# Two graph attention layers on one core: the landing of a gathered chunk awaited by each step's own chunk, on another engine

## The chip, the cores and the metric

The kernel runs on one core of one Trainium2 chip. The metric is the device time of one execution in microseconds, the median of the runs. The core has TensorE (PE), VectorE (DVE), ScalarE (ACT), GpSimd (POOL) and SyncE (SP), each with an instruction queue of its own, and they wait for each other by semaphores. Sixteen DMA engines move data between HBM and the on-chip memories, SBUF and PSUM.

## The reference

There are 3125 nodes with 128 features and 50000 edges (src, dst), sorted by dst. The dst are drawn as the whole part of 3125 u², u uniform, so low nodes have many edges and high ones few. Two layers of the same form follow each other, and at the end a layer norm over x + out:

```python
q = (x @ qw + qb).reshape(N, 2, 128); k, v likewise
alpha = einsum('ehd,ehd->eh', q[dst], k[src]) / sqrt(128)
ex = exp(alpha - segment_max(alpha, dst)[dst])
w = ex / (segment_sum(ex, dst)[dst] + 1e-16)
out = segment_sum(w * v[src], dst).mean(heads) + x @ sw + sb + x @ lin_w + lin_b
```

## The kernel before

Edges are taken in 391 chunks of 128, nodes in 49 groups of 64 (half bins), two of which make a tile of 128 nodes. A step pairs one chunk with one group. Since dst is sorted, the pairs that hold edges form a staircase, where each step goes on either by one chunk or by one group: 391 + 48 pairs, and a layer has 440 steps. So the chunk of step t is t minus the group of step t. Group, tile, chunk and ring slot of each step are computed from dst on the chip, as rows of 440 values (`bin_i`, `tile_i`, `slot_i`), and are read into registers eight at a time: by PE the tiles (`tiles_of`, L291) and slots (`slots_of`, L298), by DVE the slots and half bins.

A layer runs like this:

- POOL gathers the 128 source rows of each chunk from HBM by an indirect DMA (L445) into the ring `gathered`, 118 chunks deep. The increments of gather n go to one of eight semaphores (`got`). Gather c of a layer waits until c - 118 + 49 sums of the layer are done (`u_ready`), so that a slot is free whatever group its chunk was last used with.
- PE multiplies a one-hot matrix of the destinations (`hot_t`) with the table of the step's tile of nodes, in three bf16 parts (`step_t`, L715), which gives each edge its transformed query row in PSUM. The bank is one of three, and is free when the dots of three steps earlier are done.
- DVE takes the dot of that row with the gathered row, once for each head, with a sum into `alpha` (`step_alpha`, L1009). For step t, while t is below 391, it first waits for the landing of chunk t, not of the chunk that the step uses.
- The steps are cut into ten blocks (26, 36, 46, five of 50, 46, 36 steps). After each the maximum by node is found by a scan over a few slots, with small pieces on PE, DVE and ACT.
- Behind the scan ACT makes the weighted one-hot matrix `whot` from `apart` (L546; `apart` itself is made by ACT at L530, in about one step of six by DVE at L1020), PE multiplies it with the gathered chunk (`step_u`, L726), and DVE adds the product to the sums of the group (`step_add`, L1040). These sums lag the dots by the size of a block and nine slots, 45 slots at first and 59 later.

All engines walk over the same list of slots, written out by the generator `slots()`. A slot holds the dots of one step `a`, a piece of a scan if one is due, and the sums that are due. In a slot PE does first the matmuls of step a + 1, then the scan's piece, then the sums. The last slots of a layer have sums only. Then the nodes are normalised and projected, layer 1's result is stored to `h_rows` in HBM, and layer 2 gathers from there.

The one-hot matrices `hot_t` come from rows of local destinations. These are stored once into HBM by SP (`store_rows`, L371, ten DMAs in three sets) and then spread over all 128 partitions, eight steps at a time, by 55 DMAs a layer (`dl_bc`, L386). SP issues each of them as soon as the one-hot matrices of two spreads earlier are made, and then issues the stores of `h_rows` and of the output.

Of the kernel before, what the change touches and what calls it, by code (L numbers as in the profile page):

```python
# [26 lines left out]
P = 128  # L27
# [13 lines left out]
RING = 118  # L41
# [15 lines left out]
LATE_ROWS, LATE_DST, LATE_MASKS = 1, 6, 7  # L57
NGR = -(-BINS // G)
# [20 lines left out]
def program(nc, A, out):  # L79
# [8 lines left out]
    with ctx:  # L88
# [92 lines left out]
        tile_i = sb("tile_i", [1, STEPS], i32)  # L181
# [74 lines left out]
        dl_in = [sem(f"dl_in{k}") for k in range(2)]  # L256

# [30 lines left out]

        def tiles_of(etype, step):

            _, v = nc.values_load_multi_w_load_instructions(  # L291
                tile_i[0:1, step:step + RB], engines=[etype], min_val=0, max_val=BINS - 1,
                skip_runtime_bounds_check_because="half of a step's half bin, within 0..24 by the staircase")
            return v
# [15 lines left out]

        def newest(t):

            return min(t, CHUNKS - 1)
# [25 lines left out]
        def made(l, c, dve):  # L339

            return l * by_dve.count(dve) + by_dve[:c + 1].count(dve)

        @block.sync
        def _(sp):
# [27 lines left out]
            dl_flat = dl_d.rearrange("(o s) e -> o (s e)", o=1)  # L373
            per_layer = STEPS // BC
            for l in range(2):
                for q in range(per_layer):
                    n = l * per_layer + q
                    if l == 0 and q == 2:
                        for w in range(1, ROW_SETS):
                            store_rows(w)  # L380
                    if n >= 2:
                        sp.wait_ge(S["hot_t_ready"], n - 1)
                    w = BLOCK_OF[(q + 1) * BC - 1] // G
                    if l == 0 and (q == 0 or w != BLOCK_OF[q * BC - 1] // G):
                        sp.wait_ge(rows_out[w], 16 * len(range(G * w, min(G * (w + 1), NBLK))))
                    sp.dma_start(dl_bc[:, n % 2, :],  # L386
                                 dl_flat[:, q * BC * P:(q + 1) * BC * P].to_broadcast([P, BC * P])
                                 ).then_inc(dl_in[n % 2], 16)
# [63 lines left out]
        def _(act):  # L452
# [72 lines left out]

            def far_apart(l, c):

                if l * STEPS + c >= UN:
                    act.wait_ge(S["whot_ready"], l * STEPS + c - UN + 1)
                nc.scalar.activation(apart[:, c % UN, :], col_b[:, 0:HB], ACT.Square,  # L530
                                     bias=ndl_e[:, c:c + 1]).then_inc(S["apart_act"], 1)
# [18 lines left out]
            for l in range(2):  # L550
                for k in range(T_AHEAD + 1):
                    split(l, k)
                for t, (a, s, cs) in enumerate(slots()):
                    if l == 0:
                        for w in range(1, ROW_SETS):
                            if a == LATE_ROWS + 2 * w - 1:
                                row_set(w)
                    if a is not None and a + T_AHEAD + 1 <= BINS:
                        split(l, a + T_AHEAD + 1)
                    k = None if a is None else a - LATE_MASKS - 2  # L560
                    if k is not None and 0 <= k < BINS:
# [40 lines left out]
        def _(pe):  # L602
# [104 lines left out]
            def step_t(l, t, b):  # L707
# [4 lines left out]
                if n >= NB:  # L712
                    pe.wait_ge(S["alpha_ready"], n - NB + 1)
                for part in range(3):
# [46 lines left out]
            for l in range(2):  # L761
# [3 lines left out]
                for t, (a, s, cs) in enumerate(slots()):  # L765
                    if l == 0:
                        late_prepare(a)
                    if a is not None:
# [3 lines left out]
                        for k in range(a + PE_AHEAD if a else 0, min(a + PE_AHEAD + 1, STEPS)):  # L772
# [8 lines left out]
                            step_t(l, k, b[k % RB])  # L781
# [58 lines left out]
        def _(dve):  # L840
# [62 lines left out]
            step(V.tensor_scalar(tile_i[:, :], bin_i[:, :], 1, None, ALU.arith_shift_right))  # L903
            V.scalar_tensor_tensor(out=odd, in0=tile_i[:, :], scalar=-2.0, in1=bin_i[:, :], op0=ALU.mult, op1=ALU.add
# [3 lines left out]
            V.tensor_copy(bq_wide, bq[:, 0, 0:1].to_broadcast([P, P])).then_inc(S["bq_ready"], 1)  # L908
            V.tensor_copy(slot_i[:, :], bank_r[96:97, 0:STEPS])
# [323 lines left out]
```

## Time and profile before

| | |
|---|---|
| median of 3 runs | 1259.71 us (1258.82 to 1260.03) |
| profiled execution | 1261.61 us, its span 1259.6 us |
| busy share of the span: PE, PEld | 78%, 53% |
| DVE, ACT, POOL | 73%, 56%, 60% |
| chain that ended last: PE, issue, POOL, DMA, DVE | 24%, 20%, 19%, 16%, 15% |
| granted TensorE clock, mean over the span | 0.851 |

The table's busy shares are averages over stages with different limits. Layer 1's gathers run from 5.9 to 503.4 us and layer 2's from 633.4 to 1125.1 us; in between and at the end POOL has nothing to do. The chain is followed back from the last instruction, at each step to what released it; "issue" in it is time in which an engine waited for nothing that the profile shows. The granted clock is 1 at 2.4 GHz and 0.5 at 1.2 GHz; values between are means over a stretch that has both.

### The profile page before, as it was taken

How to read it: one execution, taken by the hardware profiler on the slowest of the kernel's cores; microseconds unless marked ns; L12 is line 12 of the kernel's file. 1: busy time of each engine (PE TensorE's matmuls, PEld its weight loads, DVE VectorE, ACT ScalarE, POOL GpSimd, SP SyncE). 2: the span in 40 equal slices, each digit the busy share in tenths (PEclk: the TensorE clock that was granted, in tenths of full speed). 3: DMA queues.
4: the chain of work that ended last, by engine and by line, in shares of the span. 5: the costliest groups of instructions: out<-in, count | busy, mean ns of one | idle time of the engine just before them, and what ended most of it. 6: DMA issues, size and time to landing. Idle time of an engine off the chain costs nothing.

```text
span 1259.6 us, 30148 instructions
## 1 busy us (share of the span) xinstructions
PE 979.8 (78%) x5388; PEld 673.2 (53%) x5388; DVE 917.1 (73%) x5514; ACT 702.1 (56%) x2724; POOL 754.2 (60%) x804
## 2 busy tenths in 40 slices
PE   4867887887687778888987677777777877778877
PEld 2635555555454545666754454545554555456655
DVE  5698887767676767888586666676667676778876
ACT  1455665646464647676264353546465646576655
POOL 7777777777777777000067777777777777750000
PEclk9988889778878988788896787888798879898788
DMA  5333323333233323000132222222233232220001
GB/s 136 88 76 87 94 81 88 84 79 78 79 79 79 85 73 86 29 2 1 43 102 81 78 78 78 79 78 81 77 87 77 80 79 79 78 77 18 1 2 51
DMA packets 52791, 88.49 MB, mean 70 GB/s; under 512 B 16787, under 2 KB 25257, under 8 KB 52617
## 3 DMA queue, kind: packets, MB, share of 16 engines
q0 software_dynamic: 25024, 51.30, 15.9%
q1 hardware_dynamic: 25001, 34.20, 9.3%
q10 hardware_dynamic: 2592, 1.07, 0.3%
q8 instruction: 61, 1.00, 0.3%
q14 instruction: 113, 0.93, 0.2%
HBM read 83.16 MB, written 3.35 MB: 69 GB/s over the span
## 4 chain that ended last, share of the span: by engine, by line
PE 24%; issue 20%; POOL 19%; DMA 16%; DVE 15%; ACT 3%; DVEq 3%; SPq 0%; POOLq 0%; ACTq 0%
POOL gathered L445 19%; PE ps L726 9%; PE ps L715 8%; DMA gathered<-in_x,src_e 8%; DMA gathered<-h_rows,src_e 8%; DVE junk L1009 6%; DVE acc L1040 4%; PE ps L824 2%; ACT whot L546 2%; PE ps L819 1%; PE ps L808 1%; DVEq L1040 1%; PE ps L703 1%; DVE apart L1020 1%; DVEq L1009 1%
## 5 line engine op out<-in xcount | busy, mean ns | idle before, releaser
L715 PE MATMUL ps<-table,hot_t 128*128 x2640 | 523.6, 313 | 136.5 <-DVE junk L1009 105.1
L1009 DVE SCALAR_TENSOR_TENSOR junk<-ps,gathered 128x129 f32<-128x129 f32 x1760 | 439.7, 288 | 248.1 <-issue 144.4
L546 ACT ACTIVATE whot<-apart,below 128x64 f32<-128x64 bf16 x1760 | 491.4, 335 | 227.5 <-DVE apart L1020 190.6
L726 PE MATMUL ps<-gathered,whot 128*128 x1760 | 457.6, 351 | 79.5 <-ACT whot L546 42.8
L445 POOL DMA_INDIRECT gathered<-in_x,src_e x391 | 376.6, 963 | 121.7 <-issue 80.8
L445 POOL DMA_INDIRECT gathered<-h_rows,src_e x391 | 372.8, 953 | 119.0 <-issue 76.8
L715 PEld LDWEIGHTS ps<-table,hot_t 128*128 128x128 bf16 x2640 | 285.6, 108 | 269.2 <-issue 204.7
L726 PEld LDWEIGHTS ps<-gathered,whot 128*128 128x128 f32 x1760 | 311.2, 222 | 193.2 <-issue 137.5
L1040 DVE TENSOR_TENSOR acc<-ps,acc 128x129 f32 x880 | 253.3, 288 | 23.2 <-PE ps L726 11.1
L530 ACT ACTIVATE apart<-col_b,ndl_e 128x64 bf16<-128x64 bf16 x652 | 217.1, 333 | 0.0
L1009 DVE DVE_READ_ACCUMULATOR junk<-ps,gathered 128x1 f32 x1760 | 144.7, 82 | 0.3
L436 POOL MEMSET gathered<- 128x118 f32 x1 | 0.3, 309 | 129.7 <-DMA h_rows<-table 129.7
L515 ACT COPY a_row<-ps 50x256 f32<-50x256 f32 (+3 forms) x20 | 7.3, 366 | 94.3 <-PE ps L735 94.3
L1020 DVE TENSOR_SCALAR apart<-ncol_b,ndl_e 128x64 bf16<-128x64 bf16 x228 | 56.0, 246 | 0.1
L997 DVE TENSOR_SCALAR hot_t<-dl_bc,part_f 128x1024 bf16<-128x1024 bf16 x110 | 54.2, 492 | 1.1 <-issue 1.1
L523 ACT COPY below<-ps 128x100 f32<-128x100 f32 (+3 forms) x20 | 4.7, 233 | 59.8 <-PE ps L757 59.8
L519 ACT ACTIVATE shrink<-drop 2x1 f32<-2x1 f32 x20 | 4.0, 202 | 57.4 <-DVE drop L1067 57.4
L824 PEld LDWEIGHTS ps<-wv,gathered 128*128 128x128 f32 x200 | 26.6, 213 | 10.8 <-issue 10.6
L692 PE MATMUL ps<-qk,xT 128*128 128x258 f32 x100 | 31.7, 403 | 0.6 <-ACT xT L587 0.6
L509 ACT CAST table<-left 128x258 bf16<-128x258 f32 x50 | 20.4, 407 | 16.5 <-DVE left L942 14.4
L824 PE MATMUL ps<-wv,gathered 128*128 128x128 f32 x200 | 29.4, 305 | 0.0
L942 DVE TENSOR_TENSOR left<-ps,table 128x258 f32<-128x258 f32 x50 | 21.1, 422 | 6.7 <-issue 3.4
(184 smaller groups left out, 571.1 us busy)
## 6 DMA issues: line engine op xcount, KB each, us to landing
dl_bc<-local_dst_rows SPq DMA_DIRECT2D x110, 256.0 KB
gathered<-in_x,src_e POOLq DMA_INDIRECT x391
gathered<-h_rows,src_e POOLq DMA_INDIRECT x391
h_rows<-table SPq DMA_DIRECT2D x6, 256.0 KB, 2.3
out<-x_rows SPq DMA_DIRECT2D x6, 256.0 KB
table<-in_L_gnn_q_w ACTq DMA_DIRECT2D x2, 128.0 KB
table<-in_L_gnn_k_w ACTq DMA_DIRECT2D x2, 128.0 KB
wv<-in_L_gnn_v_w ACTq DMA_DIRECT2D x2, 128.0 KB
```

Of the source, the lines that this page charges most:

```text
L445: nc.gpsimd.indirect_dma_start(out=gathered[:, c % RING, 0:F], out_offset=None, in_=rows[:, :], in_offset=bass.IndirectOffsetOnAxis(ap=src ...
L530: nc.scalar.activation(apart[:, c % UN, :], col_b[:, 0:HB], ACT.Square, bias=ndl_e[:, c:c + 1]).then_inc(S["apart_act"], 1)
L546: last = nc.scalar.activation(whot[:, c % UN, h * HB:(h + 1) * HB], apart[:, c % UN, :], ACT.Exp, scale=FAR, bias=below[:, j % 2, h, o:o + 1])
L692: nc.tensor.matmul(bank_u[n % NB][:, 0:CW], xT[:, k * P:(k + 1) * P], qk[:, l, :], start=True, stop=False)
L715: last = nc.tensor.matmul(bank_t[n % NB][:, 0:CW], hot_t[:, n // BC % 2, t % BC, :], table[:, bass.ds(b, 1), part, :].rearrange("p o c -> ...
L726: nc.tensor.matmul(bank_u[n % NB][:, 0:C1], whot[:, c % UN, :], gathered[:, bass.ds(slot, 1), :].rearrange("p o c -> p (o c)"), start=True ...
L824: last = nc.tensor.matmul(o, uT[q % 2][:, h, t * P:(t + 1) * P], wv[:, l, h * F:(h + 1) * F], start=False, stop=(t == k - 1 and h == HEADS ...
L942: V.tensor_tensor(left[:, n % 2, :], bank_u[n % NB][:, 0:CW], table[:, k, 0, :], ALU.subtract).then_inc(S["left_ready"], 1)
L997: V.tensor_scalar(hot_t[:, q % 2, :, :].rearrange("p k e -> p (k e)"), dl_bc[:, q % 2, :], part_f[:, 0:1], None, ALU.is_equal).then_inc(S[ ...
L1009: last = V.scalar_tensor_tensor(out=junk[:, t % 2, h, :], in0=bank_t[n % NB][:, h * C1:(h + 1) * C1], scalar=1.0, in1=gathered[:, bass.ds( ...
L1020: V.tensor_scalar(apart[:, c % UN, :], ncol_b[:, 0:HB], ndl_e[:, c:c + 1], None, ALU.not_equal).then_inc(S["apart_dve"], 1)
L1040: V.tensor_tensor(bin_acc, bank_u[n % NB][:, 0:C1], bin_acc, ALU.add).then_inc(S["u_added"], 1)
```

## The change

A step waits for the landing of its own chunk, on PE, before its matmuls; DVE doesn't wait for landings any more. SP waits for each gather in order and counts the landings on one semaphore a layer (`landed`). The count that a step needs, min(chunk, 390) + 1, is computed on DVE beside the tile, both stored as pairs in `tile_i`, and PE loads 16 words at once instead of 8; an AND with 511 makes the value for the wait. SP no longer issues the spreads but the first two: ACT does, at each eighth slot, two spreads ahead. In layer 1 SP relays the first eight landings before the stores of the second and third set of rows. The ring has 114 slots instead of 118. The AND leaves the value as it is.

```diff
-RING = 118
+RING = 114
+EARLY_CHUNKS = 8
...
-        tile_i = sb("tile_i", [1, STEPS], i32)
+        tile_i = sb("tile_i", [1, STEPS, 2], i32)
+        landed = [sem(f"landed{l}") for l in range(2)]
...
             _, v = nc.values_load_multi_w_load_instructions(
-                tile_i[0:1, step:step + RB], engines=[etype], min_val=0, max_val=BINS - 1,
...
-            return v
+                tile_i[0:1, step:step + RB, :].rearrange("o s v -> o (s v)"), engines=[etype], min_val=0, max_val=CHUNKS,
...
+            return [(v[2 * k].with_bounds(min_val=0, max_val=BINS - 1), (v[2 * k + 1] & 511).with_bounds(min_val=1, max_val=CHUNKS)) for k in range(RB)]
...
+        def spread_rows(eng, n):
+
+            q = n % per_layer
+            eng.dma_start(dl_bc[:, n % 2, :], dl_flat[:, q * BC * P:(q + 1) * BC * P].to_broadcast([P, BC * P])
+                          ).then_inc(dl_in[n % 2], 16)
...
+            sp.wait_ge(rows_out[0], 16 * G)
+            for n in range(2):
+                spread_rows(sp, n)
             for l in range(2):
-                for q in range(per_layer):
-                    n = l * per_layer + q
-                    if l == 0 and q == 2:
+                for c in range(CHUNKS):
+                    n = l * CHUNKS + c
+                    if l == 0 and c == EARLY_CHUNKS:
                         for w in range(1, ROW_SETS):
                             store_rows(w)
-                    if n >= 2:
-                        sp.wait_ge(S["hot_t_ready"], n - 1)
...
+                    sp.wait_ge(got[n % GQ], 16 * (n // GQ + 1))
+                    sp.sem_inc(landed[l], 1)
...
+            def spread_ahead(l, a):
+
+                n = l * per_layer + a // BC + 2
+                if n < 2 * per_layer:
+                    act.wait_ge(S["hot_t_ready"], n - 1)
+                    if l == 0 and n < per_layer:
+                        w = BLOCK_OF[(n + 1) * BC - 1] // G
+                        if w != BLOCK_OF[n * BC - 1] // G:
+                            act.wait_ge(rows_out[w], 16 * len(range(G * w, min(G * (w + 1), NBLK))))
+                    spread_rows(act, n)
...
                     if a is not None and a + T_AHEAD + 1 <= BINS:
                         split(l, a + T_AHEAD + 1)
+                    if a is not None and a % BC == 0:
+                        spread_ahead(l, a)
...
-            def step_t(l, t, b):
+            def step_t(l, t, b, count):
...
                 if n >= NB:
                     pe.wait_ge(S["alpha_ready"], n - NB + 1)
+                pe.wait_ge(landed[l], count)
...
+            V.tensor_copy(tile_i[:, :, 0], slot_i[:, :])
...
+            V.tensor_scalar(tile_i[:, :, 1], bank_r[64:65, 0:STEPS], float(CHUNKS - 1), 1.0, ALU.min, ALU.add)
...
             def step_alpha(l, t, slot):
                 n, j = l * STEPS + t, BLOCK_OF[t]
-                m = l * CHUNKS + newest(t)
                 if n >= 2:
                     dve.wait_ge(S["alpha_ready"], n - 1)
-                if t == newest(t):
-                    dve.wait_ge(got[m % GQ], 16 * (m // GQ + 1))
                 dve.wait_ge(S["t_ready"], n + 1)
```

## Rows read from the trace of the kernel before

**Rows 1.** The page: busy tenths of POOL in 40 slices of the span.

```profile
POOL 7777777777777777000067777777777777750000
```

**Rows 2.** Timeline of POOL around the gathers' ends and beginning: start us, us, instruction.

```profile
501.19 0.94 POOL L445 DMA_INDIRECT gathered<-in_x,src_e  x1 [0.30 <-issue]
502.44 0.94 POOL L445 DMA_INDIRECT gathered<-in_x,src_e  x1 [0.30 <-issue]
...
633.45 0.95 POOL L445 DMA_INDIRECT gathered<-h_rows,src_e  x1
...
1124.19 0.94 POOL L445 DMA_INDIRECT gathered<-h_rows,src_e  x1 [0.30 <-issue]
```

**Rows 3.** Windows of the dots, L1009: stretch, its us, DVE busy (records), clock, DMA.

```profile
80.00:200.00 120.00, 64.28 (x519) 0.91 0.33 88
200.00:500.00 300.00, 122.67 (x964) 0.85 0.30 80
500.00:560.00 60.00, 27.38 (x216) 0.86 0.08 23
1120.00:1181.00 61.00, 28.20 (x220) 0.92 0.08 24
```

**Rows 4.** Waits from 200 to 500 us: in total us, times, longest.

```profile
ACT whot L546 <- DVE apart L1020: 60.8, 27, 4.3
...
DVE junk L1009 <- issue: 52.1, 70, 2.4
...
DVE junk L1009 <- PE ps L715: 15.1, 32, 0.9
```

**Rows 5.** Timeline of DVE: each layer's last dots, and layer 2's first.

```profile
558.81 0.29 DVE L1009 SCALAR_TENSOR_TENSOR junk<-ps,gathered 128x129 f32<-128x129 f32 x1
...
638.13 0.29 DVE L1009 SCALAR_TENSOR_TENSOR junk<-ps,gathered 128x129 f32<-128x129 f32 x1 [0.32 <-PE ps L715]
...
1179.97 0.29 DVE L1009 SCALAR_TENSOR_TENSOR junk<-ps,gathered 128x129 f32<-128x129 f32 x1
```

**Rows 6.** Timeline of DVE: the last long stand before a dot in layer 1.

```profile
502.49 0.29 DVE L1009 SCALAR_TENSOR_TENSOR junk<-ps,gathered 128x129 f32<-128x129 f32 x1 [1.55 <-issue]
```

**Rows 7.** Timeline of PEld, 506 to 512.4 us: weight loads of steps and one sum.

```profile
507.07 0.58 PEld L715 LDWEIGHTS ps<-table,hot_t 128*128 128x128 bf16 x3
...
508.14 0.58 PEld L715 LDWEIGHTS ps<-table,hot_t 128*128 128x128 bf16 x3
...
509.98 0.32 PEld L715 LDWEIGHTS ps<-table,hot_t 128*128 128x128 bf16 x3
...
510.54 0.32 PEld L715 LDWEIGHTS ps<-table,hot_t 128*128 128x128 bf16 x3
...
512.06 0.30 PEld L726 LDWEIGHTS ps<-gathered,whot 128*128 128x128 f32 x2 [0.65 <-issue]
```

**Rows 8.** PE's sequencer by line: ns min/median/max, first and last start us.

```profile
L291 PEldq TENSOR_LOAD <-tile_i x110: 587/591/772, 39.3 to 1166.8; - x110
...
L715 PEldq FUSED_REGOPS  x2640: 46/46/46, 40.9 to 1178.4; - x189
...
L713 PEldq EVENT_SEMAPHORE  x149: 51/51/987, 46.2 to 1171.9; - x149
```

**Rows 9.** The chain that ended last, one piece: start us, us, what.

```profile
498.70 1.88 DMA gathered<-in_x,src_e
```

**Rows 10.** DMA issues on SP's and ACT's sequencers by line: ns min/median/max.

```profile
L386 SPq DMA_DIRECT2D dl_bc<-local_dst_rows x110: 319/320/601, 34.0 to 1147.0; - x110
...
L455 ACTq DMA_DIRECT2D table<-in_L_gnn_q_w x2: 451/452/454, 0.7 to 3.2; - x2
```

**Rows 11.** Windows, all engines: us, busy PE, PEld, DVE, ACT, POOL.

```profile
200.00:500.00 300.00, 234.04 (x1258) 156.59 (x1256) 211.29 (x1375) 171.30 (x697) 227.17 (x240) 0.85 0.30 80
```

**Rows 12.** Timeline of POOL in layer 1: the longest stand for sums.

```profile
175.54 0.94 POOL L445 DMA_INDIRECT gathered<-in_x,src_e  x1 [1.95 <-PE ps L726]
```

**Rows 13.** Windows of the sums' matmuls, L726 on PE: two records a sum.

```profile
100.00:156.00 56.00, 23.75 (x94) 0.91 0.33 90
```

More of the change, by code:

```diff
@@ L291, in tiles_of @@
             _, v = nc.values_load_multi_w_load_instructions(
-                tile_i[0:1, step:step + RB], engines=[etype], min_val=0, max_val=BINS - 1,
-                skip_runtime_bounds_check_because="half of a step's half bin, within 0..24 by the staircase")
-            return v
+                tile_i[0:1, step:step + RB, :].rearrange("o s v -> o (s v)"), engines=[etype], min_val=0, max_val=CHUNKS,
+                skip_runtime_bounds_check_because="a step's tile of nodes, within 0..24 by the staircase, and the number of "
+                                                  "chunks up to its own, 1..CHUNKS")
+            return [(v[2 * k].with_bounds(min_val=0, max_val=BINS - 1), (v[2 * k + 1] & 511).with_bounds(min_val=1, max_val=CHUNKS)) for k in range(RB)]
         def slots_of(etype, step):
@@ L309, in by_head @@
             return t.rearrange("p (i h n) -> p i h n", h=HEADS, n=HB)
-        def newest(t):
-            return min(t, CHUNKS - 1)
         def slots():
@@ L341, in made @@
             return l * by_dve.count(dve) + by_dve[:c + 1].count(dve)
+        dl_flat = dl_d.rearrange("(o s) e -> o (s e)", o=1)
+        per_layer = STEPS // BC
+        def spread_rows(eng, n):
+            q = n % per_layer
+            eng.dma_start(dl_bc[:, n % 2, :], dl_flat[:, q * BC * P:(q + 1) * BC * P].to_broadcast([P, BC * P])
+                          ).then_inc(dl_in[n % 2], 16)
         @block.sync
@@ L372, in _ @@
             store_rows(0)
-            dl_flat = dl_d.rearrange("(o s) e -> o (s e)", o=1)
-            per_layer = STEPS // BC
+            sp.wait_ge(rows_out[0], 16 * G)
+            for n in range(2):
+                spread_rows(sp, n)
             for l in range(2):
-                for q in range(per_layer):
-                    n = l * per_layer + q
-                    if l == 0 and q == 2:
+                for c in range(CHUNKS):
+                    n = l * CHUNKS + c
+                    if l == 0 and c == EARLY_CHUNKS:
                         for w in range(1, ROW_SETS):
                             store_rows(w)
-                    if n >= 2:
-                        sp.wait_ge(S["hot_t_ready"], n - 1)
[L383 to L388, printed above, removed]
+                    sp.wait_ge(got[n % GQ], 16 * (n // GQ + 1))
+                    sp.sem_inc(landed[l], 1)
                 if l == 0:
@@ L780, in _ @@
                                 pe.wait_ge(S["part3"], l * BINS + k + 1)
-                            step_t(l, k, b[k % RB])
+                            step_t(l, k, *b[k % RB])
                     if s is not None:
@@ L902, in _ @@
             step(V.tensor_tensor(bin_i[:, :], step_f[0:1], bank_r[64:65, 0:STEPS], ALU.subtract))
-            step(V.tensor_scalar(tile_i[:, :], bin_i[:, :], 1, None, ALU.arith_shift_right))
-            V.scalar_tensor_tensor(out=odd, in0=tile_i[:, :], scalar=-2.0, in1=bin_i[:, :], op0=ALU.mult, op1=ALU.add
+            step(V.tensor_scalar(slot_i[:, :], bin_i[:, :], 1, None, ALU.arith_shift_right))
+            V.tensor_copy(tile_i[:, :, 0], slot_i[:, :])
+            V.scalar_tensor_tensor(out=odd, in0=slot_i[:, :], scalar=-2.0, in1=bin_i[:, :], op0=ALU.mult, op1=ALU.add
                                    ).then_inc(S["odd_ready"], 1)
@@ L908, in _ @@
             V.tensor_copy(bq_wide, bq[:, 0, 0:1].to_broadcast([P, P])).then_inc(S["bq_ready"], 1)
+            V.tensor_scalar(tile_i[:, :, 1], bank_r[64:65, 0:STEPS], float(CHUNKS - 1), 1.0, ALU.min, ALU.add)
+            dve.wait_ge(S["odd_ready"], 1)
             V.tensor_copy(slot_i[:, :], bank_r[96:97, 0:STEPS])
```

## Prediction

> **What bounds the kernel now.** I read the slices first. POOL is busy for the same seven tenths of every slice of both layers but the first and the last [rows 1]. It does one thing there: 391 gathers in a layer, each 0.94 us with 0.30 us before the next, so one chunk of 128 edges every 1.25 us (502.44 - 501.19) [rows 2]. In layer 1 the last starts at 502.44; in layer 2 the first starts at 633.45 and the last at 1124.19, which is 490.74 / 390 = 1.258 us each [rows 2].
>
> Then the windows of the attention dots (L1009; four records make a step: two dots, two accumulator reads). From 200 to 500 us 964 / 4 = 241 steps ran in 300 us, 1.245 us each: the gather's pace to the last per cent [rows 3]. In that stretch DVE stood before a dot for 52.1 us on "issue" (it has no releaser in the profile; the landing wait at the head of `step_alpha` is what stands there) and only 15.1 us on TensorE [rows 4]. When the gathers are over, 500 to 560 still hold 216 / 4 = 54 steps, and 1120 to 1181 another 55 [rows 3]. The last dots are at 559.0 and 1180.2 (ends 559.1 and 1180.3) [rows 5].
>
> That is the whole matter. Step t waits for chunk min(t, 390), so 391 steps run at the gather's pace and 49 follow it. A step's own chunk is t minus its group. With dst spread as 3125 u², group = 49 (c/391)² to a good estimate, so the step that uses chunk c is c + 49 (c/391)². The steps could therefore end when the gathers end.
>
> **The compute's own pace, p.** It decides how much of this comes back. Three measures: (500 to 559.1 less the 1.55 us stall at 502.49) / 54 = 1.07 us; 60 / 55 = 1.09, its first part still waiting for chunks; 80 to 200 us, where the gathers were ahead, 519 / 4 = 130 steps in 120 us, 0.92 us, but with few sums at its start [rows 3, 5, 6]. I take 1.05 before the change. It isn't TensorE's alone: a step with its sum starts every 0.56 us at the upper clock, 2.4 GHz (510.54 - 509.98), and every 1.07 us at the lower, 1.2 GHz (508.14 - 507.07) [rows 7]. It is mostly DVE's chain, with TensorE at its side in the low stretches (granted clock 0.85 from 200 to 500 and 0.86 in the free stretch, so I change nothing for the clock) [rows 3].
>
> **The change, part by part.**
>
> *The register work on PE* (added). Eight steps have one load of 8 words, 591 ns on PE's sequencer; a register operation is 46 ns, a semaphore event 51 ns [rows 8]. Now 16 words are loaded (no row has such a load: from nothing more, up to twice, +0.59 us per 8 steps = 0.074 a step), one AND a step (0.046) and one wait a step (0.051). Bounds: 0 if all of it lies under the array's work, 0.17 if none does. TensorE has 0.5 us of slack in a step at the upper clock, but a lump can open a gap there: the weights of the sum at 512.06 come 0.65 us late, about the length of one load, with nothing else named [rows 7]. On the whole it lies nearer to hidden. I take 0.03: p = 1.08.
>
> The Trainium skill, "Runtime: NRT & Kernel Launch", "Instruction fetch mechanics", says a register load costs about 200 ns per register. That would make the 8 words here 1.6 us. The row says 0.591 for all eight, so the trace disagrees; what that rule would give stands among the rivals.
>
> *The wait moved from DVE to PE.* Behind it on PE are the three matmuls of the step, the scan's transposes and the sum of the same slot; DVE waits for those. The price is latency, not pace: the dot comes a step matmul (0.5 us) later behind its chunk. From the start of a gather to its dot I allow 3.5 us: 1.88 us from the gather's start to the release of DVE at 500.58 as the chain has it [rows 9], SP's relay, 0.5 and 0.45 for matmuls and dots.
>
> *SP relays landings.* 782 waits and increments, at about the price of an event each, against 1.25 us between chunks: nothing, under the gathers. In layer 1 the relay stops ahead of chunk 8 for six row stores, which at 0.32 us an issue [rows 10] are 2 us, once, and step 8 waits then for much else: nothing, at most 2 us.
>
> *The 108 row spreads move to ACT.* On SP one took 0.32 us, on ACT a DMA issue takes 0.45 [rows 10]: 49 us in all, 0.056 a step. ACT was busy 171 of 300 us from 200 to 500 and stood 61 us for DVE before its exponentials [rows 4, 11], so its slack covers it: I take 0; if ACT were the bound it would be 0.056. The spreads come 9 steps ahead of use instead of being sent at once, some 10 us: enough unless the queue is blocked.
>
> *The ring, 118 to 114.* Chunk c now waits for c - 65 sums instead of c - 69. In the steady part a sum lags its step by 55 to 59 slots, so the gather may run 7 to 11 chunks ahead of the step number, and the step's own chunk is older by the group: no stop. Only in layer 1, where the gathers are ahead, does it act. At 175.54 POOL had already stood 1.95 us for the sums [rows 12]. Chunk 114 (issued at about 155 by counting back from 390) now needs 49 sums; by 156 there are 94 / 2 = 47 [rows 13], and after that about one each 1.25 us. Carried through with one gather each 1.25 us, the gathers come out some 2 us later (four chunks, 5 us, at worst; 0 at best): +2 in layer 1.
>
> *DVE's prologue*: two small vector operations, no more than 1 us, beside the loading of weights: 0.
>
> **The sum.** A layer's last dot comes at the largest of: (start of gather c) + 3.5 + p (440 - c - 49 (c/391)²), over c; and in layer 1, where 241 + 54 = 295 steps come after 200 us [rows 3], 200 + p × 295. The largest c is where 1.25 / (1 + c/(4 × 391)) falls to p; for 1.08, c = 246.
> Layer 2: 633.45 + 246 × 1.258 + 3.5 + 1.08 × 174.6 = 1135.1, 45.2 us before 1180.3. Layer 1: 322.6 (gather 246: 502.44 - 144 × 1.249) + 2 + 3.5 + 188.6 = 516.7 by the gathers and 200 + 318.6 = 518.6 by the compute; the later counts, 40.5 us before 559.1. What follows the last dot (74.4 us to the first gather of layer 2, 79.3 to the end) is compute in the order of the slots and stays.
> Together 85.7 us. The profiled execution took 1261.6 us (2.0 outside its span) and the median is 1.9 below it: 1261.6 - 85.7 - 1.9 = 1174.0.
>
> **By p, the same sum:** 1.00 gives 1156 (all gather-bound); 1.05 gives 1164; 1.12, 1194; 1.15, 1210; 1.22, 1255. It breaks even at 359.1 / 295 = 1.22 in layer 1 and 542.2 / 440 = 1.23 in layer 2.
>
> **Rivals.**
> 1. *PE's sequencer isn't hidden at all* (the load doubled, AND and wait bare): p = 1.05 + 0.17 = 1.22, 1255 us. With the load alone bare and its time in proportion to its words, p = 1.05 + 0.074 = 1.12 and the time 1194, still inside my range. For it: the gap of 0.65 us in rows 7. Against: it is the only gap in those rows, and at the lower clock the steps there follow each other without one. Anything from 1210 to 1257: 0.08.
> 2. *Slower.* The register lump and ACT's DMA issues both lie bare on the step's chain: p = 1.22 + 0.056 = 1.28; 200 + 378 = 577.6 and 638.1 + 563 = 1201.3, so 18.5 + 21 us later: 1299. It decides where p passes 1.23. 0.05, of which 0.02 for a load whose added words cost far more than the first eight, of which rows 8 show nothing.
>    That last is the Trainium skill's rule of 200 ns a register ("Runtime: NRT & Kernel Launch"): a step would get 0.20 and the bare AND and wait 0.10, p = 1.35, an estimate of 1351 us; no run here shows such a load.
> 3. *The ring takes the place of the wait.* If sums stall at every block's end (nine a layer) and hold POOL for four chunks, 5 us each time, up to 45 us a layer go: 1175 to 1260. For it: rows 12. Against: layer 2's gathers came every 1.258 us on the mean of all 391 [rows 2], which leaves no room for such stands. 0.03.
> 4. *The change doesn't do it*: another wait keeps steps at 1.25 (ACT's spreads late, relay blocked): no change, 0.01.
>
> Forecast, p between 1.00 and 1.15: 0.80, range 1155 to 1210, likeliest 1174. Below 1155 (no ring cost, shorter latency): 0.03. Over 1257 by rival 2: 0.05. A measurement of this kernel tells 0.2% (2.5 us) from no change. So faster: 0.80 + 0.03 + 0.08 + 0.03 = 0.94, same 0.01, slower 0.05.
>
> **What would show it.** Steps per 20 us in the windows should rise from 16 to 17 early and 19 or 20 near a layer's end; the last dot of a layer should stand 5 to 15 us behind the last gather, not 56; gathers keep 1.25 us. DVE's stands on "issue" should shrink, and PE get stands at the landing wait. Near 200 us POOL should stand a few us more for sums. If steps keep 1.2 us or more where gathers are ahead, p was wrong: look for gaps on PE each eighth step. If POOL has new stands, the ring was.

## The result, and the profile after

The changed kernel takes 1199.99 us, the median of four runs (1199.13 to 1201.07). The kernel before took 1259.26 in four runs beside them (1257.84 to 1260.03). The ratio is 0.9531, with a 95% interval from 0.9514 to 0.9547: 59.3 us less. The forecast was 1174, with a range of 1155 to 1210. The time lies inside the range, but the gain is 59 us where 86 was forecast (1174.0 against 1259.7), and most of what follows is about these 26 us.

In the listing of the changed kernel the dots are L1028, the step matmuls L734, the sums' matmuls L745, the sums on DVE L1059, the gather L450, and SP's relay L393. The span is 1197.9 us. First the windows of the dots, L1028 (stretch, its us, DVE busy and records, clock, DMA share, GB/s), which answer to [rows 3]:

```profile
80.00:200.00 120.00, 58.47 (x467) 0.87 0.31 78
200.00:500.00 300.00, 140.79 (x1108) 0.93 0.33 85
```

Four records are a step. From 200 to 500 us the kernel made 277 steps where it had made 241: 1.083 us each, no longer the gather's 1.25. From 80 to 200 us it made 117 where it had made 130. So the change gives a faster middle and a slower beginning.

The timeline of DVE, the last dot of each layer, against [rows 5]:

```profile
533.53 0.29 DVE L1028 SCALAR_TENSOR_TENSOR junk<-ps,gathered 128x129 f32<-128x129 f32 x1
...
1118.14 0.29 DVE L1028 SCALAR_TENSOR_TENSOR junk<-ps,gathered 128x129 f32<-128x129 f32 x1
```

And the timeline of POOL: the gathers after the longest stands, the last of layer 1, and the first and the last two of layer 2, against [rows 2, 12]:

```profile
164.95 0.94 POOL L450 DMA_INDIRECT gathered<-in_x,src_e  x1 [13.43 <-PE ps L745]
...
184.49 0.94 POOL L450 DMA_INDIRECT gathered<-in_x,src_e  x1 [2.52 <-PE ps L745]
...
517.05 0.94 POOL L450 DMA_INDIRECT gathered<-in_x,src_e  x1 [0.30 <-issue]
...
609.84 0.95 POOL L450 DMA_INDIRECT gathered<-h_rows,src_e  x1
...
1099.20 0.94 POOL L450 DMA_INDIRECT gathered<-h_rows,src_e  x1 [0.30 <-issue]
1100.45 0.94 POOL L450 DMA_INDIRECT gathered<-h_rows,src_e  x1 [0.30 <-PE ps L745]
```

Layer 1's last dots end at 533.8 instead of 559.1, 25.3 us earlier. Layer 2's last dots begin 508.3 us after its first gather, where it was 546.5 (1179.97 - 633.45) [rows 2, 5]: 38.2 us less. What lies between and behind took 1.8 us more, and the span is 61.7 us shorter. The last dot stands 16.5 and 17.7 us (1118.14 - 1100.45) behind the start of the last gather, where it stood 56.4 and 55.8; I had said 5 to 15. Gathers still come at the same pace (490.61 / 390 = 1.258 us in layer 2). But in layer 1 the last one starts at 517.05, 14.6 us later than before, where I had allowed 2. POOL stands 13.43 us for a sum before the gather at 164.95, and 1.86, 0.50, 0.66 and 2.52 before four others up to 184.49.

The waits over the whole span (total us, times, longest). Rows 4 have only the stretch from 200 to 500 us, so here is the kernel before's line over its whole span:

```profile
DVE junk L1009 <- issue: 144.4, 206, 2.5
```

and the changed kernel's:

```profile
PEld ps L734 <- issue: 173.7, 207, 8.2
...
DVE junk L1028 <- PE ps L734: 116.1, 178, 1.8
...
POOL gathered L450 <- PE ps L745: 69.0, 169, 13.4
...
PE ps L734 <- SPq L393: 56.0, 73, 2.2
PE ps L734 <- DVE junk L1028: 53.4, 64, 1.2
...
DVE junk L1028 <- issue: 36.5, 89, 0.8
```

DVE's stands without a releaser fell from 144.4 to 36.5 us. DVE has no landing wait any more, so these 36.5 us are something else, and a part of the 144.4, and of the 52.1 in [rows 4], may have been too. The landing wait is now PE's, 56.0 us behind SP's relay, and DVE stands for the matmuls instead.

PE's, SP's and ACT's sequencers by line (ns min/median/max, first and last start us), against [rows 8, 10]:

```profile
L294 PEldq TENSOR_LOAD <-tile_i x110: 1101/1105/1292, 37.9 to 1104.4; - x110
...
L732 PEldq ALU_OP  x880: 32/32/42, 39.5 to 1116.2; - x176
...
L393 SPq EVENT_SEMAPHORE  x782: 17/17/17, 33.0 to 1103.2; - x196
...
L350 ACTq DMA_DIRECT2D dl_bc<-local_dst_rows x108: 326/326/363, 39.4 to 1090.8; - x108
```

The load of 16 words takes 1105 ns, where 8 words took 591. The AND is 32 ns, the relay 17 ns, a spread on ACT 326 ns where I had allowed 450.

### The profile page after: what moved, and what is told of

It is laid out like the page before. It is cut to its first block, busy times and chain, and to the rows that moved or that the text cites. A ratio compares the mean times of both kernels' runs of the same rounds, so it can differ in the third digit from the quotient of the medians.

```text
span 1197.9 us, 31804 instructions
## 1 busy us (share of the span) xinstructions
PE 935.5 (78%) x5388; PEld 647.9 (54%) x5388; DVE 926.4 (77%) x5516; ACT 714.5 (60%) x2724; POOL 752.6 (63%) x804
## 3 DMA queue, kind: packets, MB, share of 16 engines
q8 instruction: 64, 1.05, 0.3%
## 4 chain that ended last, share of the span: by engine, by line
PE 27%; issue 20%; POOL 19%; DVE 18%; DMA 10%; DVEq 3%; ACT 2%; SPq 0%; ACTq 0%; POOLq 0%
POOL gathered L450 19%; PE ps L745 11%; PE ps L734 9%; DVE junk L1028 9%; DMA gathered<-h_rows,src_e 6%; DVE acc L1059 4%; DMA gathered<-in_x,src_e 3%; PE ps L843 2%; ACT whot L562 2%; PE ps L827 1%; PE ps L838 1%; DVEq L1028 1%; DVEq L1059 1%; DVE apart L1039 1%; PE ps L721 1%
## 5 line engine op out<-in xcount | busy, mean ns | idle before, releaser
L562 ACT ACTIVATE whot<-apart,below 128x64 f32<-128x64 bf16 x1760 | 497.7, 336 | 171.7 <-DVE apart L1039 93.1
L734 PE MATMUL ps<-table,hot_t 128*128 x2640 | 499.9, 302 | 126.6 <-SPq L393 56.0
L1028 DVE SCALAR_TENSOR_TENSOR junk<-ps,gathered 128x129 f32<-128x129 f32 x1760 | 439.6, 287 | 161.6 <-PE ps L734 116.1
L745 PE MATMUL ps<-gathered,whot 128*128 x1760 | 445.4, 343 | 89.6 <-ACT whot L562 46.1
L450 POOL DMA_INDIRECT gathered<-in_x,src_e x391 | 375.0, 959 | 137.9 <-issue 82.2
L450 POOL DMA_INDIRECT gathered<-h_rows,src_e x391 | 372.7, 953 | 118.9 <-issue 82.3
L745 PEld LDWEIGHTS ps<-gathered,whot 128*128 128x128 f32 x1760 | 294.6, 211 | 206.8 <-issue 142.4
L734 PEld LDWEIGHTS ps<-table,hot_t 128*128 128x128 bf16 x2640 | 275.0, 104 | 242.8 <-issue 173.7
L1059 DVE TENSOR_TENSOR acc<-ps,acc 128x129 f32 x880 | 253.6, 288 | 36.3 <-PE ps L745 24.3
L1028 DVE DVE_READ_ACCUMULATOR junk<-ps,gathered 128x1 f32 x1760 | 143.8, 82 | 0.5
L511 ACT CAST table<-ps 128x258 bf16<-128x258 f32 x50 | 18.6, 371 | 19.6 <-PE ps L711 16.5
```

Of the source, the lines that this page charges most:

```text
L450: nc.gpsimd.indirect_dma_start(out=gathered[:, c % RING, 0:F], out_offset=None, in_=rows[:, :], in_offset=bass.IndirectOffsetOnAxis(ap=src ...
L562: last = nc.scalar.activation(whot[:, c % UN, h * HB:(h + 1) * HB], apart[:, c % UN, :], ACT.Exp, scale=FAR, bias=below[:, j % 2, h, o:o + 1])
L734: last = nc.tensor.matmul(bank_t[n % NB][:, 0:CW], hot_t[:, n // BC % 2, t % BC, :], table[:, bass.ds(b, 1), part, :].rearrange("p o c -> ...
L745: nc.tensor.matmul(bank_u[n % NB][:, 0:C1], whot[:, c % UN, :], gathered[:, bass.ds(slot, 1), :].rearrange("p o c -> p (o c)"), start=True ...
L1028: last = V.scalar_tensor_tensor(out=junk[:, t % 2, h, :], in0=bank_t[n % NB][:, h * C1:(h + 1) * C1], scalar=1.0, in1=gathered[:, bass.ds( ...
L1059: V.tensor_tensor(bin_acc, bank_u[n % NB][:, 0:C1], bin_acc, ALU.add).then_inc(S["u_added"], 1)
```

## Experiments

There were twelve runs of nine different kernels; three kernels ran twice (r5 and r11, r6 and r9, r7 and r10). Each median stands beside runs of the kernel before on the same chip. A kernel that waits on constants takes the chunk numbers from a table `OWN` of 440 numbers, worked out for this input's dst (the step's own chunk, plus one); for another dst it would wait for the wrong chunk. The kernel before took 1259.3 us beside r1 to r4 and 1256.9 beside r9 to r11, on two chips. The other five ran on two more chips, on which the kernel before itself took 1683.4 (r5 to r8) and 1680.7 (r12); they have a section of their own. Differences between a run of the first group and one of the second carry the 2.4 us between their kernels before.

### Ring, register work and the moved parts

**r1: the kernel before with the smaller ring.**

```diff
-RING = 118
+RING = 114
```

> The kernel before with the ring at 114 and nothing else. The changed kernel's trace shows POOL standing 13.4 us for sums at about 151 us, where I had allowed 2 us in all. Theory ring: the four rows are worth their four gathers where the gathers are ahead, so this kernel is 2 to 5 us slower than before (1261 to 1264) and POOL stands some 5 us more near 155 us. Theory pace: the 13.4 us come mostly from slower steps ahead of it, and here, with the old pace, POOL stands 2 us more at most and the time is 1259 to 1261.

1264.25 us, ratio 1.0046 (1.003 to 1.0061), 4.9 us more. The timeline of POOL shows where:

```profile
156.70 0.95 POOL L445 DMA_INDIRECT gathered<-in_x,src_e  x1 [4.27 <-PE ps L726]
```

This is the place that the prediction named: chunk 114, about 155 us.

**r2: the changed kernel with its wait on constants.** No counts, no AND, and the load has 8 words again.

```diff
-        tile_i = sb("tile_i", [1, STEPS, 2], i32)
+        tile_i = sb("tile_i", [1, STEPS], i32)
...
-                            step_t(l, k, *b[k % RB])
+                            step_t(l, k, b[k % RB], OWN[k])
```

> The changed kernel, but PE waits for the landing count as a constant written into the program (the own chunk of each step for these data), loads 8 words for 8 steps and has no AND. Everything else as changed, ring 114. Theory pace (the register work on PE is the loss: a load of 1105 ns for 591, an ALU operation of 32 ns a step): steps with the gathers ahead go back towards 0.93 to 0.97 us, POOL's stands near 155 to 190 us fall from 18 to 5 us or less, and the time is 1180 to 1190. Theory place (the loss is that PE stands at the landing wait ahead of the sums, or ACT's DMA issues): 1196 to 1201, as the changed kernel.

1182.3 us, ratio 0.9404 (0.9374 to 0.9434). So the counts in registers cost 17.7 us in all (1199.99 - 1182.3), against a wait on a constant.

**r3: r2 with the ring of 118.**

> As the run before it, with the ring back at 118. Theory ring: another 4 to 8 us less than with 114, from fewer stands of POOL in layer 1 alone; layer 2 the same length. Rival: the same within 2 us, because with the quicker steps the gathers don't reach the ring's end for long.

1177.27 us, ratio 0.9358 (0.9329 to 0.9387). The ring of 114 costs 5.0 us here too (1182.3 - 1177.27). The gathers after the longest stands, r2's first:

```profile
160.28 0.94 POOL L450 DMA_INDIRECT gathered<-in_x,src_e  x1 [8.42 <-PE ps L745]
```

and r3's:

```profile
160.16 0.95 POOL L450 DMA_INDIRECT gathered<-in_x,src_e  x1 [3.43 <-PE ps L745]
```

**r4: r3 with the old criterion.** The relay, ACT's spreads and the wait on PE stay, but step t waits for chunk min(t, 390) again.

```diff
-                            step_t(l, k, b[k % RB], OWN[k])
+                            step_t(l, k, b[k % RB], min(k, CHUNKS - 1) + 1)
```

> As the run before it, but the constant is that of the kernel before: step t waits on PE for chunk min(t, 390). It has all that was moved (wait on PE, relay by SP, spreads by ACT) and none of the own-chunk rule. If the own-chunk rule is the whole gain, the time is that of before or up to 4 us more (1259 to 1264: the dot comes one step's matmuls later behind its chunk, once a layer). If the moved parts cost pace, it shows at the ends of the layers, where no gather binds: 49 steps each with 0.05 to 0.1 us more would be 5 to 10 us.

1269.55 us, ratio 1.0096 (1.0063 to 1.0128). So the moved parts by themselves cost 10.2 us (1269.55 - 1259.32; the profiled executions are 6.7 apart), and the criterion alone is worth 92.3 us (1269.55 - 1177.27).

**r10: the changed kernel with the 16-word load, but waiting on constants.** The pairs are loaded and only the tile is used: no AND, no wait on a register.

```diff
-            return [(v[2 * k].with_bounds(...), (v[2 * k + 1] & 511).with_bounds(...)) for k in range(RB)]
+            return [v[2 * k].with_bounds(min_val=0, max_val=BINS - 1) for k in range(RB)]
```

> The same kernel as the seventh run (16-word load, waits on constants, ring 114). Theory load: 1192 to 1196, two thirds of the way from 1182.3 to 1200.0. Rival (the AND and the wait on a register are the loss): 1183 to 1186.

1199.11 us, ratio 0.9532 (0.9505 to 0.9559). The longer load alone is 16.8 of the 17.7 us (1199.11 - 1182.3); the 880 ANDs and waits on a register are 0.9 (1199.99 - 1199.11), which is within the error of both. They take the place of something: in r10 the wait on a constant leaves 880 records of EVENT_SEMAPHORE on PE's sequencer, 51 ns each, where the changed kernel has 880 of ALU_OP, 32 ns each, and no record of the wait (31,661 and 31,804 instructions in all). I had expected the load to be two thirds. The gather behind the longest stand:

```profile
164.29 0.94 POOL L451 DMA_INDIRECT gathered<-in_x,src_e  x1 [13.19 <-PE ps L746]
```

It stands as long as in the changed kernel (13.43), and 4.8 us longer than in r2. The longer load makes the stand longer; the smaller ring is the other part of it (8.42 against 3.43).

**r9: r3 with the wait back on DVE,** for the step's own chunk, through the relay.

```diff
-                pe.wait_ge(landed[l], count)
...
+                dve.wait_ge(landed[l], OWN[t])
                 dve.wait_ge(S["t_ready"], n + 1)
```

> The same kernel as the sixth run (constants, ring 118, the wait for the landing on DVE), which ran on a chip where the kernel before took 1683 us. On a chip where it takes 1259: theory place, 1166 to 1171 (some 8 us from the 1177.3 with the wait on PE); rival (ACT's issues and the relay cost those 10 us), 1175 to 1179.

1170.99 us, ratio 0.931 (0.9284 to 0.9335), the fastest of all. Placing the wait on PE costs 6.3 us (1177.27 - 1170.99; 6.0 by the profiled spans, 1174.4 and 1168.4). Its dots, L1027, in windows as above:

```profile
80.00:200.00 120.00, 65.15 (x524) 0.90 0.35 90
200.00:500.00 300.00, 141.54 (x1119) 0.90 0.33 85
```

131 steps from 80 to 200 us, as many as before: the slow beginning is gone. But from 200 to 500 it made 280, 1.07 us each. This is not the compute alone. Steps still wait for their own chunks here:

```profile
DVE junk L1027 <- issue: 25.4, 40, 2.2
...
DVE junk L1027 <- SPq L393: 10.2, 19, 1.1
```

These are the waits from 200 to 500 us; DVE stood 10.2 us behind SP's relay and 25.4 without a releaser.

**r11: the count worked out on PE.** A load of 8 words (the half group), and for each step the tile by a shift and the chunk by a subtraction and an AND.

```diff
-                            step_t(l, k, *b[k % RB])
+                            step_t(l, k, (b[k % RB] >> 1).with_bounds(...), ((k + 1 - b[k % RB]) & 511).with_bounds(...))
```

> The same kernel as the fifth run (8 half bins loaded, tile and count by register arithmetic, ring 118). On the other chip it was 4% slower than the kernel before, as the one with the most instructions on PE. If the load of 16 words is the loss: 1178 to 1184. If register operations and the register wait are: 1190 or more.

1298.8 us, ratio 1.0311 (1.0279 to 1.0344): slower than the kernel before. It differs from r3 in this arithmetic and the register wait (SP's last increment of a layer is also 50 instead of 1, so that the spare step passes), and is 121.5 us slower (1298.8 - 1177.27), 0.138 us for each of the 880 steps. The theory that the length of the load is all had expected about r3's time, and fell. The rows that its sequencer on PE adds, and two of its waits:

```profile
L723 PEldq ALU_OP  x1760: 43/44/53, 41.4 to 1218.5; - x196
...
L723 PEldq MOVE  x880: 29/29/33, 41.3 to 1218.3; - x176
```

```profile
PEld ps L725 <- issue: 244.0, 735, 8.5
...
DVE junk L1017 <- PE ps L725: 188.0, 437, 2.2
```

Two ALU operations and a move are 0.117 us a step (2 x 0.044 + 0.029), and they replace r3's event of 0.051 for the wait. PE's weight loads stood without a releaser 735 times, where they did so 207 times in the changed kernel.

### Why a longer load costs: eight steps on PE

Where the gathers are ahead and the clock is at its upper level, a load of tile numbers leaves a gap ahead of one step's weights in every eight. The time from one such gap to the next is the pace of eight steps on PE; the granted clock is 1.00 in all seven stretches below. The timeline of PEld from 186 to 215 us (start, us, instruction, in brackets the idle time ahead), the kernel before:

```profile
188.07 0.34 PEld L715 LDWEIGHTS ps<-table,hot_t 128*128 128x128 bf16 x3 [0.48 <-issue]
...
194.52 0.34 PEld L715 LDWEIGHTS ps<-table,hot_t 128*128 128x128 bf16 x3 [0.50 <-issue]
```

r9, with constants and the wait on DVE:

```profile
187.19 0.34 PEld L733 LDWEIGHTS ps<-table,hot_t 128*128 128x128 bf16 x3 [0.47 <-issue]
...
193.63 0.34 PEld L733 LDWEIGHTS ps<-table,hot_t 128*128 128x128 bf16 x3 [0.50 <-issue]
```

r3, with constants and the wait on PE, ring 118 like r9:

```profile
190.96 0.34 PEld L734 LDWEIGHTS ps<-table,hot_t 128*128 128x128 bf16 x3 [0.62 <-issue]
...
197.99 0.35 PEld L734 LDWEIGHTS ps<-table,hot_t 128*128 128x128 bf16 x3 [0.58 <-issue]
```

r2, the same with ring 114:

```profile
191.44 0.34 PEld L734 LDWEIGHTS ps<-table,hot_t 128*128 128x128 bf16 x3 [0.63 <-issue]
...
198.47 0.35 PEld L734 LDWEIGHTS ps<-table,hot_t 128*128 128x128 bf16 x3 [0.58 <-issue]
```

r10, with the load of 16 words:

```profile
205.52 0.35 PEld L735 LDWEIGHTS ps<-table,hot_t 128*128 128x128 bf16 x3 [1.10 <-issue]
...
213.06 0.34 PEld L735 LDWEIGHTS ps<-table,hot_t 128*128 128x128 bf16 x3 [1.09 <-issue]
```

the changed kernel:

```profile
198.44 0.34 PEld L734 LDWEIGHTS ps<-table,hot_t 128*128 128x128 bf16 x3 [1.09 <-issue]
...
206.20 0.34 PEld L734 LDWEIGHTS ps<-table,hot_t 128*128 128x128 bf16 x3 [1.09 <-issue]
...
213.65 0.34 PEld L734 LDWEIGHTS ps<-table,hot_t 128*128 128x128 bf16 x3 [1.09 <-issue]
```

and r11:

```profile
205.29 0.34 PEld L725 LDWEIGHTS ps<-table,hot_t 128*128 128x128 bf16 x3 [0.82 <-issue]
...
214.25 0.34 PEld L725 LDWEIGHTS ps<-table,hot_t 128*128 128x128 bf16 x3 [0.81 <-issue]
```

| kernel | eight steps, us | a step |
|---|---|---|
| before | 194.52 - 188.07 = 6.45 | 0.81 |
| r9 | 193.63 - 187.19 = 6.44 | 0.81 |
| r3, a wait a step on PE | 197.99 - 190.96 = 7.03 | 0.88 |
| r2, the same, ring 114 | 198.47 - 191.44 = 7.03 | 0.88 |
| r10, 16 words | 213.06 - 205.52 = 7.54 | 0.94 |
| after, AND and register wait | 206.20 - 198.44 = 7.76; 213.65 - 206.20 = 7.45 | 0.97; 0.93 |
| r11, 8 words, two ALU operations and a move | 214.25 - 205.29 = 8.96 | 1.12 |

Seven or eight sums lie between the eight steps, which makes little difference: r10's eight steps before these, with one sum more, took 7.55 us (205.52 - 197.97).

From r2 to r10 eight steps grow by 0.51 us, and the load itself grew by 1.105 - 0.591 = 0.514. Nothing of it is hidden. The gap ahead of the weights grows by the same (0.58 to 1.09). From r9 to r3, which differ in the place of the wait alone, they grow by 0.59 us, 0.07 each; an event costs 0.051 in [rows 8]. The ring makes no difference here (r3 and r2), and neither do the AND and the register wait in the place of the constant one: the changed kernel's stretches, 7.76 and 7.45, lie on both sides of r10's. So in these stretches PE's sequencer is what a step costs, and a longer load or an added wait comes out whole. Over the whole run most of it is hidden: 110 loads with 0.51 us more each are 56 us, and r10 is 16.8 us slower than r2.

### The chips where gathers don't bound

Five kernels ran where the kernel before took 1683.4 (r5 to r8) and 1680.7 (r12). The kernel before has no trace from these chips.

r5 is r11 (the count worked out on PE, ring 118):

> No pairs in memory: PE loads the 8 half bins of 8 steps (as DVE does for its sums) and computes the tile as half bin shifted by one and the count as (step + 1 - half bin) AND 511; SP adds 49 to the count after the last chunk, so that the spare step passes. Ring 118. Theory pace by the load (the 16-word load, 514 ns more, is the loss): near the run with constants, 1178 to 1184, and safe for any data. Rival (the register arithmetic and the wait on a register are the loss): 1190 or more, since it has three ALU operations a step instead of one.

1754.21 us, ratio 1.0428 (1.039 to 1.0466).

r6 is r9 (constants, wait on DVE, ring 118):

> Constants, ring 118, but the wait for the landing count stands on DVE ahead of the dots, as in the kernel before, and not on PE. Theory place (PE standing at the landing holds up sums and matmuls that could run): faster than 1177, by some 8 to 10 us if this is what the run with the old criterion showed (1269.6 against 1259.3). Rival (the 10 us are ACT's issues of the spreads and SP's relay): 1176 to 1179, no change.

1686.79 us, ratio 1.0019 (1.0003 to 1.0034).

r7 is r10 (16-word load, constants):

> Ring 114, waits on constants, no AND, but PE loads the 16 words of pairs as the changed kernel does. Between it and the run with 8 words (1182.3) lies the load alone, between it and the changed kernel (1200.0) the AND and the wait on a register. By the durations in the trace (514 ns against 8 x 32 ns for 8 steps) two thirds of the 17.7 us should be the load: 1194. Rival: the load is hidden and the register wait is the loss, 1183 to 1186.

1705.07 us, ratio 1.0137 (1.0106 to 1.0169).

r8 is r6 with the old criterion:

```diff
-                dve.wait_ge(landed[l], OWN[t])
+                dve.wait_ge(landed[l], min(t, CHUNKS - 1) + 1)
```

> The criterion of before (chunk min(t, 390)), waited for on DVE, with SP's relay and ACT's spreads. It differs from the kernel before in the relay and the spreads alone. If ACT's issues cost the 10 us of the run with the old criterion: 1267 to 1271. If the place of the wait did: 1259 to 1261.

1690.95 us, ratio 1.0035 (1.0011 to 1.0059).

**r12: one packed word.** This one is general: tile * 512 + count in one word, a load of 8 words, `v & 511` for the wait and `v >> 9` in the address, ring 118 (the pairs need 1760 bytes more in a partition than the packed words, a ring row 516).

```diff
-            V.tensor_copy(tile_i[:, :, 0], slot_i[:, :])
...
+            step(V.tensor_scalar(tile_i[:, :], bank_r[64:65, 0:STEPS], float(CHUNKS - 1), 1.0, ALU.min, ALU.add))
+            step(V.scalar_tensor_tensor(out=tile_i[:, :], in0=slot_i[:, :], scalar=512.0, in1=tile_i[:, :], op0=ALU.mult, op1=ALU.add))
```

> A version for any data: the tile and the count packed into one 32-bit word (512 x tile + count, one more vector operation in the prologue), so that PE loads 8 words for 8 steps as before; the count is the word AND 511 as in the changed kernel, the tile is the word shifted by nine inside the address; the memory saved gives the ring its 118 rows back. Theory load (the 16-word load is the loss on PE's sequencer, the AND and the register wait are not): as with constants and ring 118, 1177 to 1180, 20 us under the changed kernel. Rival (what made the half-bin version 120 us slower than constants is the shift or the register wait): 1200 or more.

1700.76 us, ratio 1.0112 (1.0076 to 1.0148). Its waits show that this is no test of the change:

```profile
POOL gathered L450 <- PE ps L745: 465.5, 183, 148.3
PEld ps L734 <- issue: 393.2, 357, 15.7
...
PEld ps L679 <- issue: 106.1, 5, 84.7
```

POOL stands 465.5 us for sums: the gathers are late because PE is, not the other way round. PE's weight loads stand for nothing that the profile names, once for 84.7 us in the loads of L679, before a single step. The other engines stand in the prologue too, ACT once for 93.3 us on "issue". The granted clock is 0.735 over r12's span. Under these conditions a rule on which chunk to await has nothing to give (r6 against r8: 4 us), and the kernels come out nearly in the order of their instructions: 30,933 (r6 at 1687, r8 at 1691), 31,661 and 31,797 (r7 at 1705, r12 at 1701), 33,554 (r5 at 1754). What makes the engines stand there isn't shown; the supply of instructions is only a guess.

## Why the prediction was right, and where 26 us went

**Right: the bound and the criterion.** Steps waited for gathers that they didn't use. The windows now show 277 steps in 300 us instead of 241, DVE's stands on "issue" fell from 144.4 to 36.5 us in the whole span, and with every other part of the change in place the criterion alone takes 92.3 us off (r4 against r3).

**Right: what could stay as it was.** The gathers keep their pace, the compute behind each layer's last dots takes 76.0 and 79.5 us where I had 74.4 and 79.3, and the clock didn't fall; it rose (0.93 from 200 to 500 us after, 0.85 before).

**Right: ACT's spreads and SP's relay** are cheap: 326 and 17 ns. Whether they are nothing is not settled: r4 says that all moved parts cost 10.2 us, r9 against r3 says that 6.3 of them are the place of the wait (measured under the new criterion, where r4 has the old). The rest, some 4 us, has no run of its own on these chips and is no larger than the spread of r4's runs (1268.3 to 1272.2).

**Wrong: four terms of the sum,** all to the same side. The range was wide enough to hold them; the gain came out at 59.3 of the 85.7 us forecast. The 26.0 us from 1174.0 to 1200.0 divide so:

| term | I took | measured | off by |
|---|---|---|---|
| compute's pace, with relay and spreads | 1.05, which gives 1161.6 with ring 118 and no register work | r9, 1171.0 | +9.4 |
| ring | 2 us | 5.0 (r2 - r3) | +3.0 |
| wait on PE | 0 to the pace | 6.3 (r3 - r9) | +6.3 |
| register work | 10.4 (1163.6 to 1174.0) | 17.7 (after - r2) | +7.3 |

Where they lie shows when each kernel is taken by layers. The steps made by 200 us are 440 less the dots' records from there on, by four. The next column is layer 1's last dot, and the last is the time from layer 2's first gather to its last dot.

| kernel | steps by 200 us | layer 1's last dot, us | layer 2, us |
|---|---|---|---|
| before | 145.0 | 559.1 | 546.8 |
| forecast for the change | 145.0 | 518.6 | 501.7 |
| r9 | 146.3 | 513.2 | 501.8 |
| r3 (wait on PE) | 141.5 | 519.5 | 501.6 |
| r2 (and ring 114) | 141.0 | 522.3 | 503.1 |
| r10 (and 16 words) | 133.8 | 534.2 | 508.7 |
| after | 132.5 | 533.8 | 508.6 |

The term of the sum that failed in layer 1 is "200 + p × 295". Its p was nearly right, for behind 200 us the changed kernel needs 333.8 / 307.5 = 1.09 us a step, where I had 1.08. But the term lets the first 200 us stand as they were, with 145 steps done, and charges them nothing. Most of them is the part where the gathers are ahead and no wait for a chunk covers the added work: the changed kernel had made some 13 steps fewer there, which is 14 of the 15 us by which layer 1 came late.

*Pace.* With p = 1.05, ring 118 and no register work the prediction's sum has layer 1's last dot at 510.2 us and gives layer 2 497.6; r9 has 513.2 and 501.8, 3.0 and 4.2 us more. The other 2.2 us are no pace: r9's median lies 2.6 us above its profiled span, where the sum adds 0.1, and what lies between and behind the layers' dots is 0.3 shorter. Of my three measures (1.07, 1.09, 0.92) the first was the nearest, and it is also the one behind the last gather, where no step waits for a chunk. By the prediction's own sum 1.07 gives 1169.5, with the ring's 2 us or without, and r9 took 1171.0. Since r9 has the relay and the spreads too, that all of the 7.2 us are the pace isn't shown.

*Register work.* The step that failed here is "TensorE has 0.5 us of slack in a step at the upper clock", with "On the whole it lies nearer to hidden". The slack was read between two steps that follow each other (0.56 us), but over eight steps, with the load, its gap and the sums in them, the same kernel takes 6.45 us, 0.81 a step: a quarter of a microsecond, half of the slack, was already spent. The bound "up to twice" for the load was right to the size: 1.105 against 0.591 is +0.514, and I had +0.59. Only how much lies bare was wrong. Rival 1's smaller form (the load alone bare, p + 0.074) is what the runs show where the gathers are ahead; in the rest of the run most of it is hidden. It gave 1194 with the base too quick; the change lands at 1200. That the load alone makes 16.8 of the 17.7 us, and the AND and the register wait next to nothing, is measured (r10).

The Trainium skill says in "Runtime: NRT & Kernel Launch", section "Instruction fetch mechanics", that a register load is about 200 ns a register even in bulk; the page means registers loaded from HBM. By that rule 16 words would be 3.2 us, an estimate. The trace has 1.105, 64 ns for each word added to the first eight (514 / 8), so for these loads, whose source `tile_i` lies in SBUF, it doesn't hold. The floor of about 600 ns that the Trainium skill gives for such a load in "DMA: Bandwidth & Descriptors", "Latency and other measured facts", agrees with the 591 ns of eight words; the added words were not free on top of it.

*The wait on PE.* "The price is latency, not pace" failed where the gathers are ahead: there r3 needs 0.07 us a step more than r9, where I had bound the event to 0.05 and then counted it with the hidden things. By 200 us r3 is 5 steps behind, and its layer 1 ends 6.2 us later (519.45 - 513.23). In layer 2 it held: 501.6 against 501.8.

*The ring.* The place was right, the size was one step further than taken: "four chunks, 5 us, at worst" came true. With the other two terms it adds up in one place. Steps in layer 1 before chunk 114 are slower (117 from 80 to 200 us, 131 in r9), so sum 49 comes later, and POOL's stand goes from 1.95 us before to 4.27 with the ring alone (r1), 8.42 with the wait on PE (r2), 13.19 with the long load (r10) and 13.43 after. Layer 1's last gather is 14.6 us later for it. Layer 2 has no such stand: its 7 us (508.6 against 501.7) come with the ring, 1.5 (r2 - r3), and the long load, 5.6 (r10 - r2).

Side figures of the prediction that don't follow from its own sum: p = 1.00 gives 1158, not 1156; and for p = 1.28 and 1.35 layer 1 is later by the gathers (584.0 and 614.8) than by the compute that was used, so that rival 2 comes to 1304 and the estimate of 1351 to 1366. The forecast's 1174 rests on none of them; the range's lower end is nearest to the first.

**Open.** The packed word (r12) should take r3's time or a little more where the kernel before takes 1259 (1177 to 1180 expected); it never ran there. A version that beats both kernels and holds for any dst is therefore argued, not shown. r9 at 1171 shows only how much is left: 29 us of the changed kernel's time are the place of the wait, the ring, the long load and, with 0.9 us, the AND. r9 is no version for any dst: its chunk numbers are constants.

## What to carry to other kernels

Ask of every wait which data the waiting instruction really reads; where the producer has a steady rate and the consumer takes its pieces out of step with it, a count that is looked up per step can be worth far more than it costs (here 92.3 us against 17.7). But price each word and each wait on the sequencer of an engine over a whole period of its loop, not between two neighbours: here, where that engine set the pace, all of it was bare. And carry such a price through every stage of the run, the early one included, where the producer is ahead and nothing covers it. A buffer that shrinks to make room cost most while the producer was ahead, and POOL's stand there grew with everything that slowed the consumer.

## What the hardware showed

- A register load on PE's sequencer is 591 ns for 8 words and 1105 ns for 16, and where PE's sequencer sets the pace all 0.51 us of the difference comes out in eight steps (7.03 to 7.54 us).
- Register arithmetic costs more than its own records. r11's two ALU operations and move, 0.117 us a step by their records, made eight steps 1.93 us longer than r2's (8.96 - 7.03), 0.24 a step, although r2's event of 0.051 is gone. The register wait, which r11 has too, isn't the rest by itself: the changed kernel has it and an AND, and its eight steps (7.45 and 7.76 us) are as long as r10's with constants (7.54). What the rest is, the records don't name.
- The same kernel took 1257 and 1259 us on two chips and 1681 and 1683 on two others, where the traces of the kernels tried have PE standing for nothing that the profile names. A change that is worth 7% on the first (r9) is worth nothing on the second (r6: 1.0019).
- One more wait a step, on a constant, costs PE 0.07 us a step where its sequencer sets the pace (r3 against r9, 7.03 and 6.44 us for eight) and nothing where the steps wait for their chunks (layer 2: 501.6 and 501.8 us).
